# Edge weights of a tensor product kept as six blocks instead of four, and one VectorE product of 512 columns instead of two

## The chip, the cores and the metric

The kernel runs on one core of one Trainium2 chip. The metric is the device time of one execution in microseconds (us); lower is better. Several executions of the kernel before were timed, and one was recorded by the hardware profiler.

## The reference, cut to what matters

A graph of 6250 nodes and 100000 edges, sorted by destination, goes through four layers, each with a residual: a graph convolution with a mixture-of-experts feed-forward (64 experts, top 2), a SAGE layer (neighbour mean), a GCN layer, and a tensor product layer. All is float32. The change concerns the last layer and the weights of its edges:

```
h = silu(edge_scalars @ fc_w1 / sqrt(8)) * 1.679
w = h @ fc_w2 / sqrt(64)                      # 100000 x 256: blocks w_a, w_b, w_c, w_d of 64
xg0, xg1 = y0[edge_src], y1[edge_src]         # 64 and 64 x 3: one gathered row of 256
mid0 = w_a * xg0 * ea0
mid1 = w_b * sum_c(xg1[c] * ea1[c]) / sqrt(3)
mid2 = (w_c * xg0) * ea1                      # 64 x 3
mid3 = (w_d * ea0) * xg1                      # 64 x 3
agg  = segment_sum([mid0, mid1, mid2, mid3], edge_dst)   # 512 columns a node
```

## The kernel before, in words

The edges are cut into 832 windows of up to 128 edges (WINDOWS, 16 windows to a step, 52 steps), each window belonging to one tile of 125 nodes. Every layer first writes a table of 6250 rows of 256 values to HBM (`table_stage`) and then goes over the 832 windows.

`aggregate` (L628 on) does this for the first three layers. For each window GpSimd (POOL) gathers 128 rows of the table by an indirect DMA (L692), VectorE (DVE) makes the one-hot matrix of the destinations (`match`, L712), TensorE (PE) multiplies it with the gathered rows into a PSUM bank (L805), and DVE adds the bank to the node sums in SBUF (`add`, L724). The gathers run through a ring of 16 message buffers; `stage` (L705) hands POOL the indices of four windows at a time. Beside this, `aggregate` makes the edge weights of the *last* layer: in batches of 384 edges, SP loads the scalars and attributes (L865, L866), PE multiplies them (`first_product`, L781), ScalarE (ACT) applies silu (L824), PE multiplies by `fc2` (`second_product`, L788, three per batch, 256 columns each), ACT copies the result into `made`, half of it scaled by an edge attribute (`keep`, L833 and L834, 128 columns each), and SP stores `made` to `edge_rows` in HBM (L871), ROW = 260 values an edge. A batch goes with eight windows. The weights of `fc2` are loaded at the start of each `aggregate` by SP, block by block (L859), and scaled by DVE (L753, L754), for which PE waits before its first matmul. The third `aggregate` also stores its one-hot matrices to HBM (`kept_hots`, L876). The batches are spread over the three: 104 in the first, 104 in the second, the other 54 in the third.

`tensor_product_edges` (L1624 on) is the last pass over the windows. For each window:

- SP loads 128 rows of `edge_rows` into one of 6 weight buffers (L1665), and every fourth window four one-hot matrices (L1654). It waits until the product six windows back is done.
- POOL gathers 128 rows of `table3`, 256 values each, into one of 12 buffers (L1677), ahead of the others; every fourth window it waits until the products of the windows whose buffers it takes are done.
- ACT makes three scaled copies of the one-hot matrix (L1691).
- DVE forms the message of 512 columns in two products (`multiply`): L1727 makes the 2 blocks that take `xg0` (128 columns), L1729 the 6 blocks that take the three parts of `xg1` (384 columns).
- PE multiplies the message by the one-hot matrices in 8 passes (L1704, L1708), and DVE adds the bank of 512 columns to the sums (`add`, L1742).

The order on DVE is written out by `staggered`: the product of window w + 2, then the sum of window w. There are 3 message buffers and 8 banks. Sync is by semaphores set by hand; each engine runs its own list in order. Each window has the first edge that the tables give it; the last windows of the 832 have no edges left, and all of them read the same padding rows.

## Time and profile before

| | us |
|---|---|
| median of 3 runs (lowest, highest) | 6108.55 (6105.67, 6122.41) |
| the profiled execution, its own time | 6108.57 |
| its span, from the first instruction to the last | 6106.9 |
| PE, DVE, POOL, ACT busy in it | 5235.0, 3703.0, 3712.4, 1915.1 |

The stages, by the instructions of each in the trace: preparation to about 359 us, first `aggregate` to 1410, experts and batch norm to 2530, second table and `aggregate` to 3660, third to 4815, fourth table to 4932, `tensor_product_edges` from there to 6021, and the output stage to the end. The busy shares are averages over stages with different limits: what a stage is bound by is read from the windows of that stage, not from this table.

How a page is read: "busy" is the time in which an engine executes; "idle before" is the time just before an instruction in which its engine did nothing, and what ended it; "issue" means that nothing which the profile shows was waited for. PEclk is the granted TensorE clock as a share of 2.4 GHz. DMA share is the mean busy share of the 16 DMA engines; as packets of several queues can overlap, it can pass 1.00.

### The profile page before, as it was taken

The page shows a single profiled execution, that of the slowest core. Times are in us where ns is not written, and L with a number is a line of the kernel's source. Part 1 is how long each engine was busy: PE and PEld are TensorE (multiplying, and loading weights), DVE is VectorE, ACT ScalarE, POOL GpSimd, SP SyncE. Part 2 cuts the span into 40 slices and gives each one's busy share as a digit, 9 for nine tenths or more (in the row PEclk, how much of TensorE's full clock was granted, in tenths as well). Part 3 has the DMA queues.
Part 4 walks back from the last instruction along what each step waited for, and adds up shares of the span by engine and source line. Part 5 has one row for each costly group of instructions (what it writes and reads, how often), then busy time and mean ns, then how long its engine had stood idle before and what let it go on. Part 6 is the DMA issues. An engine that isn't in the chain of part 4 may idle for free. (4 is left out here: it accounts for less than half of the span.)

```text
span 6106.9 us, 94754 instructions
## 1 busy us (share of the span) xinstructions
PE 5235.0 (86%) x22327; PEld 3459.7 (57%) x22327; DVE 3703.0 (61%) x11360; ACT 1915.1 (31%) x5997; POOL 3712.4 (61%) x3961
## 2 busy tenths in 40 slices
PE   3589999996599995689999988899777689999998
PEld 2554444444388884444444445444333478888887
DVE  8746666666711112555555544555555579999997
ACT  0142222221022220422222214222000377777775
POOL 0147777771066661377777764777777557777771
PEclk9988888885799997788888877877776699999998
DMA  3145555554199993155555564666555468888884
GB/s 150 37 129 147 147 148 145 149 145 75 55 324 322 319 319 139 48 143 146 147 149 147 147 127 122 199 197 199 168 158 156 91 202 260 258 260 259 260 259 109
DMA packets 692159, 1062.44 MB, mean 174 GB/s; under 512 B 210437, under 2 KB 532051, under 8 KB 690970
## 3 DMA queue, kind: packets, MB, share of 16 engines
q0 software_dynamic: 180864, 480.03, 29.5%
q1 hardware_dynamic: 504383, 565.43, 28.9%
q10 hardware_dynamic: 6460, 12.03, 0.6%
q8 instruction: 151, 2.47, 0.2%
q14 instruction: 301, 2.47, 0.1%
HBM read 826.26 MB, written 236.47 MB: 174 GB/s over the span
## 5 line engine op out<-in xcount | busy, mean ns | idle before, releaser
L692 POOL DMA_INDIRECT agg_msg<-table,agg_idx x2496 | 2363.2, 947 | 842.5 <-issue 676.1
L805 PE MATMUL bank<-agg_msg,agg_hots 128*125 128x256 f32 (+1 forms) x4992 | 1910.9, 501 | 336.0 <-DMA agg_msg<-table,agg_idx 201.5
L805 PEld LDWEIGHTS bank<-agg_msg,agg_hots 128*125 128x125 f32 x4992 | 973.1, 228 | 1256.4 <-DVE agg_hots L712 669.3
L724 DVE TENSOR_TENSOR acc<-acc,bank 125x256 f32 x2496 | 1052.2, 422 | 1013.8 <-PE bank L805 971.3
L1677 POOL DMA_INDIRECT tp_src<-table,tp_idx x832 | 805.8, 968 | 300.2 <-issue 251.9
L1691 ACT ACTIVATE tp_hots<-tp_hot,tp_weight 128x125 f32<-128x125 f32 x2496 | 813.2, 390 | 281.2 <-PE bank L1708 238.5
L712 DVE TENSOR_SCALAR agg_hots<-iota_i,dst_w 128x126 f32<-128x126 f32 x2496 | 760.0, 305 | 0.0
L1708 PEld LDWEIGHTS bank<-tp_msg,tp_hots 128*125 128x125 f32 x4992 | 681.2, 189 | 47.1
L1708 PE MATMUL bank<-tp_msg,tp_hots 128*125 128x128 f32 x4992 | 685.8, 274 | 0.0
L833 ACT ACTIVATE agg_made<-bank,agg_made 128x128 f32<-128x128 f32 x786 | 288.6, 367 | 1255.6 <-PE bank L788 1253.3
L788 PE MATMUL bank<-agg_fc,agg_hid 64*128 64x256 f32 x1572 | 664.6, 509 | 0.0
L1742 DVE TENSOR_TENSOR acc<-acc,bank 125x512 f32 x832 | 594.0, 714 | 3.5 <-issue 1.6
L1704 PE MATMUL bank<-tp_msg,tp_hot 128*125 128x256 f32 x1664 | 559.8, 418 | 31.2 <-DVE tp_msg L1729 30.1
L1729 DVE TENSOR_TENSOR tp_msg<-tp_weight,tp_src 128x384 f32<-128x384 f32 x832 | 486.9, 585 | 0.0
L788 PEld LDWEIGHTS bank<-agg_fc,agg_hid 64*128 64x128 f32 x1572 | 278.4, 221 | 336.4 <-issue 336.4
L1511 DVE COPY ffn_res<-bank 128x256 f32<-128x256 f32 x162 | 68.8, 425 | 536.4 <-PE bank L1476 368.4
L723 DVE TENSOR_TENSOR deg_in<-deg_in,bank 125x1 f32 x832 | 130.7, 157 | 415.0 <-PE bank L805 387.2
L1428 POOL DMA_INDIRECT ffn_rows<-tokens,moe_token_of x162 | 157.7, 974 | 333.5 <-issue 333.5
L824 ACT ACTIVATE agg_hid<-bank 64x384 f32<-64x384 f32 x262 | 126.6, 483 | 724.9 <-PE bank L781 724.9
L1489 ACT ACTIVATE ffn_hid<-bank,ffn_b 128x128 f32<-128x128 f32 x648 | 184.6, 368 | 475.0 <-PE bank L1465 468.4
L1465 PE MATMUL bank<-ffn_cols,acc 128*128 128x128 f32 x2592 | 318.2, 277 | 3.0 <-DMA acc<-in_L_gnn_w_dram 2.2
L1704 PEld LDWEIGHTS bank<-tp_msg,tp_hot 128*125 128x125 f32 x1664 | 246.0, 187 | 124.1 <-issue 42.5
(285 smaller groups left out, 5407.5 us busy)
## 6 DMA issues: line engine op xcount, KB each, us to landing
tp_weight<-edge_rows SPq DMA_DIRECT2D x832, 130.0 KB
edge_rows<-agg_made SPq DMA_DIRECT2D x262, 390.0 KB, 3.5
acc<-in_L_w_laid_dram SPq DMA_DIRECT2D x162, 512.0 KB
acc<-in_L_gnn_w_dram SPq DMA_DIRECT2D x162, 512.0 KB
kept_hots<-agg_hots SPq DMA_DIRECT2D x208, 252.0 KB, 2.6
tp_hot<-kept_hots SPq DMA_DIRECT2D x208, 252.0 KB, 4.0
agg_msg<-table,agg_idx POOLq DMA_INDIRECT x2496, 2.9
table<-tab_out SPq DMA_DIRECT2D x40, 625.0 KB
```

Source lines behind the costliest of these rows:

```text
L692: pool.indirect_dma_start(out=msg[PER * g + r][:, 0:D], out_offset=None, in_=table[:, :], in_offset=bass.IndirectOffsetOnAxis(ap=idx[g][:, ...
L712: dve.tensor_scalar(hot[r % HOTS], net.iota_i[:, 0:HOT_W], net.dst_w[:, ds(WPI * i + r, 1)], None, ALU.is_equal).then_inc(s_hot, 1)
L724: dve.tensor_tensor(row, row, bank[0:P, 0:D], ALU.add).then_inc(s_add, 1)
L788: pe.matmul(wb[n % 2][:, 0:4 * MUL], hid[j % 2][:, c * Q:(c + 1) * Q], fc2[:, :, :].rearrange("p b n -> p (b n)"), start=True, stop=True). ...
L805: pe.matmul(net.bank[w % BANKS][0:P, 0:sums], hot[w % HOTS][:, 0:P], msg[w][:, :], start=True, stop=True).then_inc(s_sum, 1)
L1465: mm = pe.matmul(hidden[b % 2][:, j * Q:(j + 1) * Q], w1[b % R][:, c, j * Q:(j + 1) * Q], cols[b % 2][:, c, :], start=(c == 0), stop=(c == ...
L1677: pool.indirect_dma_start(out=src[w % R][:, :], out_offset=None, in_=table[:, :], in_offset=bass.IndirectOffsetOnAxis(ap=idx[w // WPI % 2] ...
L1691: ins = act.activation(hots[w % RM][:, c, :], hot[w // BLOCK % RB][:, w % BLOCK, 0:P], ACT.Copy, scale=weight[w % RW][:, 4 * MUL + 1 + c:4 ...
L1704: pe.matmul(out[:, 0:4, :], hot[w // BLOCK % RB][:, w % BLOCK, 0:P], m[:, 0:4, :], start=True, stop=False, skip_group_check=True)
L1708: mm = pe.matmul(out[:, 4 + c:8:3 - c, :], hots[w % RM][:, c, :], m[:, 4:6 + c:1 + c, :], start=False, stop=(c == 2), skip_group_check=True)
L1729: dve.tensor_tensor(quad, bc(wv[:, 2:4, :], 2, [Q, 2, 3, MUL]), bc(sv[:, 1:4, :], 1, [Q, 2, 3, MUL]), ALU.mult).then_inc(s_msg, 1)
L1742: dve.tensor_tensor(row, row, banks[w % len(banks)][0:P, :], ALU.add).then_inc(s_add, 1)
```

## The change

The weights of an edge are stored as six blocks of 64 instead of four, two of them twice (`fc2_of` = 0, 3, 3, 2, 1, 1), so ROW is 388 values instead of 260. With an access pattern that reads them as blocks 0, 1, 1, 2 and 3, 4, 4, 5, one product of 512 columns makes the whole message. In `aggregate`, `second_product` has 384 columns instead of 256, ACT's two copies 192 instead of 128, two more blocks of `fc2` are loaded, and the attributes stand behind the sixth block. In the first two `aggregate` the one-hot ring has 6 buffers instead of 8, each a tensor of its own, made 5 windows ahead instead of 6; in the third the ring of 16 lies in the unused half of the accumulator's tensor.

```
--- before.py
+++ after.py
@@ -54,7 +54,8 @@
...
 MUL = 64
-ROW = 4 * MUL + 4
+WIDE = 6
+ROW = WIDE * MUL + 4
 LN_EPS = 1e-5
...
@@ -635,13 +636,18 @@
...
     AHEAD = 12
-    HOTS, HOT_AHEAD = 8 if kept_hots is None else 16, 6
+    HOTS, HOT_AHEAD = (6, 5) if kept_hots is None else (16, 6)
     KEPT = HOTS // BLOCK
...
         msg = [ph.sb(f"msg{r}", [Q, sums]) for r in range(WPI)]
-        hots = [ph.sb(f"hots{r}", [Q, BLOCK, HOT_W]) for r in range(KEPT)]
-        hot = [hots[r // BLOCK][:, r % BLOCK, :] for r in range(HOTS)]
+        if kept_hots is None:
+            hot = [ph.sb(f"hot{r}", [Q, HOT_W])[:, :] for r in range(HOTS)]
+        else:
+            size = BLOCK * HOT_W
+            hots = [net.acc_full[:, T * D + r * size:T * D + (r + 1) * size].rearrange("p (b n) -> p b n", n=HOT_W)
+                    for r in range(KEPT)]
+            hot = [hots[r // BLOCK][:, r % BLOCK, :] for r in range(HOTS)]
         s_stored = [ph.sem(f"stored{r}") for r in range(KEPT)]
...
@@ -658,7 +664,7 @@
...
         first_batch, count = batches
-        fc1, fc2 = ph.sb("fc1", [8, MUL]), ph.sb("fc2", [MUL, 4, MUL])
+        fc1, fc2 = ph.sb("fc1", [8, MUL]), ph.sb("fc2", [MUL, WIDE, MUL])
         scal = [ph.sb(f"scal{b}", [8, BATCH * Q]) for b in (0, 1)]
...
@@ -666,7 +672,8 @@
...
         zb, wb = net.bank[BANKS + 1], net.bank[BANKS + 2:BANKS + 4]
-        fc2_of = (0, 2, 3, 1)
+        fc2_of = (0, 3, 3, 2, 1, 1)
+        FC_LOADS = 1 + len(fc2_of)

...
@@ -709,7 +716,7 @@
...
                         dve.wait_ge(s_stored[group % KEPT], 16 * (group // KEPT))
-                    dve.tensor_scalar(hot[r % HOTS], net.iota_i[:, 0:HOT_W], net.dst_w[:, ds(WPI * i + r, 1)], None,
+                    dve.tensor_scalar(hot[(WPI * i + r) % HOTS], net.iota_i[:, 0:HOT_W], net.dst_w[:, ds(WPI * i + r, 1)], None,
                                       ALU.is_equal).then_inc(s_hot, 1)
...
@@ -748,10 +755,11 @@
...
                 dve.sem_inc(s_add, BANKS)
-                dve.wait_ge(s_fc, 16 * 5)
-
-                dve.tensor_scalar(fc2[:, 0:3, :], fc2[:, 0:3, :], 1.679 * MUL ** -0.5, None, ALU.mult).then_inc(s_fcs, 1)
-                dve.tensor_scalar(fc2[:, 3, :], fc2[:, 3, :], 1.679 * MUL ** -0.5 * 3 ** -0.5, None, ALU.mult).then_inc(s_fcs, 1)
+                dve.wait_ge(s_fc, 16 * FC_LOADS)
+
+                dve.tensor_scalar(fc2[:, 0:4, :], fc2[:, 0:4, :], 1.679 * MUL ** -0.5, None, ALU.mult).then_inc(s_fcs, 1)
+                dve.tensor_scalar(fc2[:, 4:6, :], fc2[:, 4:6, :], 1.679 * MUL ** -0.5 * 3 ** -0.5, None,
+                                  ALU.mult).then_inc(s_fcs, 1)
                 if degrees:
...
@@ -785,10 +793,10 @@
...
                         pe.wait_ge(s_made, n - 1)
-                    pe.matmul(wb[n % 2][:, 0:4 * MUL], hid[j % 2][:, c * Q:(c + 1) * Q],
+                    pe.matmul(wb[n % 2][:, 0:WIDE * MUL], hid[j % 2][:, c * Q:(c + 1) * Q],
                               fc2[:, :, :].rearrange("p b n -> p (b n)"), start=True, stop=True).then_inc(s_w, 1)

-                pe.wait_ge(s_fc, 16 * 5)
+                pe.wait_ge(s_fc, 16 * FC_LOADS)
                 pe.wait_ge(s_fcs, 2)
...
@@ -802,7 +810,7 @@
...
                         pe.wait_ge(s_msg[w], 16 * i + 16)
-                        pe.matmul(net.bank[w % BANKS][0:P, 0:sums], hot[w % HOTS][:, 0:P], msg[w][:, :],
+                        pe.matmul(net.bank[w % BANKS][0:P, 0:sums], hot[(WPI * i + w) % HOTS][:, 0:P], msg[w][:, :],
                                   start=True, stop=True).then_inc(s_sum, 1)
...
@@ -826,12 +834,13 @@
...
                     n = BATCH * j + c
-                    to, of = (m.rearrange("p (k h n) -> p k h n", k=2, h=2)
-                              for m in (made[j % 2][:, c, 0:4 * MUL], wb[n % 2][:, 0:4 * MUL]))
+                    half = WIDE // 2 * MUL
+                    to, of = made[j % 2][:, c, :], wb[n % 2]
                     act.wait_ge(s_w, n + 1)
                     act.wait_ge(s_in[j % 2], 32 * (j // 2) + 32)
-                    act.activation(to[:, :, 0, :], of[:, :, 0, :], ACT.Copy, scale=made[j % 2][:, c, 4 * MUL:4 * MUL + 1])
-                    act.activation(to[:, :, 1, :], of[:, :, 1, :], ACT.Copy).then_inc(s_made, 1)
+                    act.activation(to[:, 0:half], of[:, 0:half], ACT.Copy,
+                                   scale=made[j % 2][:, c, WIDE * MUL:WIDE * MUL + 1])
+                    act.activation(to[:, half:2 * half], of[:, half:2 * half], ACT.Copy).then_inc(s_made, 1)

...
@@ -863,7 +872,7 @@
...
                     sp.dma_start(scal[j % 2][:, :], net.scal_t[:, rows_of(j)]).then_inc(s_in[j % 2], 16)
-                    sp.dma_start(made[j % 2][:, :, 4 * MUL:ROW],
+                    sp.dma_start(made[j % 2][:, :, WIDE * MUL:ROW],
                                  net.attr[rows_of(j), :].rearrange("(c p) k -> p c k", p=Q)).then_inc(s_in[j % 2], 16)
...
@@ -1689,7 +1698,7 @@
...
                         ins = act.activation(hots[w % RM][:, c, :], hot[w // BLOCK % RB][:, w % BLOCK, 0:P], ACT.Copy,
-                                             scale=weight[w % RW][:, 4 * MUL + 1 + c:4 * MUL + 2 + c])
+                                             scale=weight[w % RW][:, WIDE * MUL + 1 + c:WIDE * MUL + 2 + c])
                     ins.then_inc(s_hots, 1)
...
@@ -1721,13 +1730,11 @@
...
                         dve.wait_ge(s_sum, w - RM + 1)
-                    m = msg[w % RM][:, :, :]
-                    wv = weight[w % RW][:, 0:4 * MUL].rearrange("p (b n) -> p b n", n=MUL)
-                    sv = src[w % R][:, :].rearrange("p (b n) -> p b n", n=MUL)
-                    dve.tensor_tensor(m[:, 0:8:4, :], wv[:, 0:2, :], sv[:, 0:1, :].broadcast_to([Q, 2, MUL]), ALU.mult)
-                    quad = m.rearrange("p (g k) n -> p g k n", g=2)[:, :, 1:4, :]
-                    dve.tensor_tensor(quad, bc(wv[:, 2:4, :], 2, [Q, 2, 3, MUL]),
-                                      bc(sv[:, 1:4, :], 1, [Q, 2, 3, MUL]), ALU.mult).then_inc(s_msg, 1)
+                    row = weight[w % RW][:, :]
+                    overlapping = bass.AP(row.tensor, row.offset, [list(row.ap[0]), [3 * MUL, 2], [MUL, 2], [MUL, 2], [1, MUL]])
+                    sv = src[w % R][:, :].rearrange("p (h k n) -> p h k n", h=2, k=2)
+                    dve.tensor_tensor(msg[w % RM][:, :, :].rearrange("p (g h k) n -> p g h k n", g=2, h=2), overlapping,
+                                      bc(sv, 1, [Q, 2, 2, 2, MUL]), ALU.mult).then_inc(s_msg, 1)

```

## Rows read from the trace of the kernel before

**Rows 1.** Stretches: each engine's busy us and instructions, granted clock, DMA share, GB/s.
```profile
core 0: us, PE busy (x) PEld busy (x) DVE busy (x) ACT busy (x) POOL busy (x), PEclk, DMA share, GB/s
370.00:1340.00 970.00, 918.10 (x2595) 470.79 (x2594) 597.85 (x2494) 218.74 (x722) 730.63 (x772) 0.82 0.54 147
...
4300.00:4770.00 470.00, 351.31 (x756) 165.80 (x756) 252.12 (x871) 0.53 (x2) 355.47 (x377) 0.68 0.52 158
4938.00:4944.00 6.00, 5.97 (x32) 5.31 (x31) 3.85 (x10) 4.41 (x15) 4.60 (x5) 0.75 0.97 317
5000.00:5900.00 900.00, 897.51 (x5644) 779.71 (x5643) 898.77 (x2161) 689.49 (x2116) 684.79 (x707) 1.00 0.87 260
...
5965.00:6010.00 45.00, 30.77 (x151) 26.24 (x151) 25.67 (x60) 18.23 (x57) 20.48 (x22) 0.73 0.93 147
```

**Rows 2.** Timeline of DVE in the last pass: start us, us, instruction.
```profile
5499.44 0.71 DVE L1742 TENSOR_TENSOR acc<-acc,bank 125x512 f32 x1
5500.03 0.31 DVE L1727 TENSOR_TENSOR tp_msg<-tp_weight,tp_src 128x128 f32<-128x128 f32 x1
5500.23 0.58 DVE L1729 TENSOR_TENSOR tp_msg<-tp_weight,tp_src 128x384 f32<-128x384 f32 x1
5500.70 0.71 DVE L1742 TENSOR_TENSOR acc<-acc,bank 125x512 f32 x1
```

**Rows 3.** Timeline of POOL in the third aggregate.
```profile
4499.66 0.94 POOL L692 DMA_INDIRECT agg_msg<-table,agg_idx  x1 [0.30 <-issue]
4500.91 0.95 POOL L692 DMA_INDIRECT agg_msg<-table,agg_idx  x1 [0.30 <-issue]
```

**Rows 4.** Timeline of POOL in the last pass, near its start and in its middle.
```profile
4955.36 0.94 POOL L1677 DMA_INDIRECT tp_src<-table,tp_idx  x1 [0.30 <-issue]
4956.61 0.94 POOL L1677 DMA_INDIRECT tp_src<-table,tp_idx  x1 [0.30 <-issue]
...
5499.40 0.96 POOL L1677 DMA_INDIRECT tp_src<-table,tp_idx  x1 [0.30 <-issue]
5500.67 0.97 POOL L1677 DMA_INDIRECT tp_src<-table,tp_idx  x1 [0.30 <-issue]
```

**Rows 5.** All gathers of the last pass: duration ns min/median/max, first and last start; landing.
```profile
L1677 POOL DMA_INDIRECT tp_src<-table,tp_idx x832: 940/964/1200, 4932.8 to 6005.7; - x167
...
DMA to landing us min/median/max: 3.2/4.0/16.0
```

**Rows 6.** Waits between 5000 and 5900 us: us in total, times, longest.
```profile
POOL tp_src L1677 <- issue: 215.2, 706, 0.3
ACT tp_hots L1691 <- PE bank L1708: 206.0, 694, 0.9
...
PE bank L1704 <- DVE tp_msg L1729: 1.5, 5, 0.6
...
DVE tp_msg L1727 <- DMA tp_src<-table,tp_idx: 0.3, 1, 0.3
```

**Rows 7.** Timeline of PE's weight loads in the last pass.
```profile
5501.25 0.84 PEld L1708 LDWEIGHTS bank<-tp_msg,tp_hots 128*125 128x125 f32 x6
5502.20 0.29 PEld L1704 LDWEIGHTS bank<-tp_msg,tp_hot 128*125 128x125 f32 x2
```

**Rows 8.** DMA between 5000 and 5900 us.
```profile
DMA packets 161021, 233.57 MB, mean 260 GB/s; under 512 B 25416, under 2 KB 138277, under 8 KB 160887
...
q1 hardware_dynamic: 126968, 139.43, 51.4%
q0 software_dynamic: 33919, 92.66, 34.9%
```

**Rows 9.** A stretch of the experts stage (columns as in Rows 1).
```profile
1662.00:1682.00 20.00, 17.08 (x105) 15.08 (x106) 2.87 (x8) 5.74 (x17) 7.49 (x10) 0.86 1.03 411
```

**Rows 10.** Costliest groups that the edge weights take in the three aggregates.
```profile
L833 ACT ACTIVATE agg_made<-bank,agg_made 128x128 f32<-128x128 f32 x786 | 288.6, 367 | 1255.6 <-PE bank L788 1253.3
L788 PE MATMUL bank<-agg_fc,agg_hid 64*128 64x256 f32 x1572 | 664.6, 509 | 0.0
```

**Rows 11.** The first aggregate's start: SP's loads of fc2, then DVE's first sum.
```profile
358.74 2.43 SPq L859 DMA_DIRECT2D agg_fc<-in_L_gnn_fc_w_dram  x4
...
365.20 0.42 DVE L724 TENSOR_TENSOR acc<-acc,bank 125x256 f32 x1
```

## The prediction

> **What bounds the kernel now.** I read the busy shares of stretches first [rows 1]. Between 5000 and 5900 us, inside the last pass, DVE is busy 898.77 of 900 us and PE 897.51, while 707 windows pass: 900 / 707 = 1.273 us a window. Both look full, so the next view is the timeline of DVE [rows 2]: from the start of one sum (L1742) to the first product 0.59 us, from that to the second product 0.20, from that to the next sum 0.47; together 1.26 to 1.27, and no gap. A DVE instruction of 512 columns holds the next one back 0.59 to 0.60, one of 128 columns 0.20, one of 384 columns 0.47. That is 64 + columns, divided by 0.96 a ns: 0.600, 0.200, 0.467, sum 1.267. Nobody delays DVE: in those 900 us it waited 0.3 us for a gather, and PE waited for it [rows 6]. PE has a little room: its weight loads of one window end at 5502.09 and the next begin at 5502.20, 0.11 us later, which leaves PE about 1.27 - 0.11 = 1.16 us of its own a window [rows 7]. So DVE sets the pace, PE comes with 1.16.
>
> Two resources stand just below that pace. The first is **POOL**. In the third aggregate a gather takes 0.94 to 0.95 us, then POOL is idle 0.30 waiting for nothing that the profile shows, and the next begins 1.25 us after the last [rows 3]. That holds where DVE, PE and the DMA engines all have room: DVE busy 252 of 470 us, DMA share 0.52, and POOL still does 377 gathers in 470 us, 1.247 us each [rows 1]. So 1.25 us is POOL's own cost of a gather, and all three aggregates are bound by it. In the last pass POOL begins with the same 1.25 and then goes 1.27 [rows 4]; it looks idle 0.30 before each of the 706 gathers, but those are the same 0.30 [rows 6]. POOL is nearly full too, and has 0.023 us to give. The second is the **DMA engines**: share 0.87 at 260 GB/s [rows 1].
>
> **The change, part by part.** The sum is made against the profiled execution's own 6108.57 us (span 6106.9 and 1.7 around it); the median is 6108.55, the same.
>
> 1. *One product instead of two.* By the rule read above, two instructions hold DVE 0.200 + 0.467 = 0.667 us, one of 512 columns 0.600. DVE's own window falls from 1.267 to 1.200, 0.067 less. The pattern has five dimensions and overlaps, which no row shows; the bounds are that it runs at the rate of the others (0.600) or gives everything back (0.667). I take 0.600, since both products of today already read with repeats and keep that rate.
> 2. *What is late next.* POOL, at 1.25. DVE overtakes it: today's lead of some windows is used up at 0.05 us a window, and from then on DVE waits for the gather. The steady part loses 1.273 - 1.250 = 0.023 us a window and not 0.067. It has the windows from 4937 to 5965 us, 1028 / 1.273 = 808: **-18.6 us**. PE's 1.16 lies below 1.25, and ACT's three copies are busy 689.49 / 707 = 0.98 us a window [rows 1]; both stay covered.
> 3. *Bytes of the last pass.* Today 233.57 MB / 707 = 330 kB a window [rows 8]. A row grows by 128 values, so a window by 128 x 512 B = 65.5 kB, to 396 kB. At 1.25 us that is 317 GB/s. What can the engines do? The lower bound is today's share taken as full use: 260 / 0.87 = 299 GB/s, which gives 1.32 us a window. The upper is the experts stage, 411 GB/s in packets of another size, 0.96 us [rows 9]. Nearest is the start of this very pass, where the queues were full of the same kinds of packets: 317 GB/s at a share of 0.97, so 327, or 1.21 us [rows 1]. I take this one: DMA stays just below POOL, at zero cost. The number of instructions on SP is the same.
> 4. *The padding windows.* From 5965 to 6010 us the DMA share is 0.93 at only 147 GB/s, and the engines wait for data [rows 1]. The other 24 windows fall mostly here, with 24 x 65.5 kB = 1.57 MB more. At 147 GB/s that is 10.7 us; at 317 GB/s 5.0; if the slow part is only the gathers of one repeated row, near 0. I take **+5**, ends 0 and +11.
> 5. *The aggregates, DMA.* Stores grow from 390 to 582 kB a batch; at a share of 0.54 [rows 1] that is hidden, except at the end of the first two, whose last windows gather a repeated row as well. Ends 0 and +7 each; I take 2 each, **+4**.
> 6. *The aggregates, PE and ACT.* L788 goes from 256 to 384 columns. Half of 509 ns [rows 10] for six passes a batch is 1.5 us in the 10 us that eight windows take. PE is idle only 970 - 918 = 52 of 970 us, 0.5 in 10, but that is at a granted clock of 0.82; the same work at 1.00 would leave 18% more, 1.8 us. Without the weights (4300 to 4770) PE is busy 351 of 470 us at 0.68, and POOL goes at the same pace [rows 1], so slack on PE does not speed the pass. The ring of 16 messages takes up the stretches at the low clock. I take 0; if that cover fails, 1.0 us a batch of 262 is open, +260 at the very worst. ACT's copies get 64 columns more, on an engine busy 219 of 970 us: 0.
> 7. *The aggregates' start.* Two more loads of fc2 at 2.43 / 4 = 0.6 us each on SP [rows 11] delay PE's first matmul by 1.2 us, three times; the loads of scalars and attributes queue behind them. POOL has 12 gathers to do before it needs the first sum, 12 x 1.25 = 15 us from about 359, and the first sum is at 365.2 [rows 11]: hidden, 8 us to spare; without it, 3.6 us in all.
> 8. *The one-hot rings.* Six buffers, made five windows ahead: PE can be at most four banks ahead of DVE's sums, so it asks for nothing that isn't made. The wait on the stored groups in the third stays as it was. 0.
>
> Sum: 6108.6 - 18.6 + 5 + 4 = **6099 us**. With every small cost at zero 6090; with them at their ends (-18.6 + 11 + 14) 6115.
>
> **The rivals.** About 0.3%, 18 us, is what a measurement of this kernel can tell from no change.
>
> *A. As above, POOL takes over.* 6090 to 6115. For it: the even 1.25 in 2496 gathers of the aggregates. Chance 0.57; in a fifth of it the costs come out at zero and the time falls just under 6090.
>
> *B. The gathers are held back by the longer product.* POOL starts at 1.25 in this pass and then falls into step with DVE: at 5500.67 a gather begins just where the second product gives DVE free (5500.23 + 0.47 = 5500.70), and its duration has gone from 0.94 to 0.97 [rows 2, 4]. No aggregate shows that, where DVE has no instruction with two inputs in SBUF. So something in a gather waits for the products. Today the two leave a seam between them; one of 0.600 us has none. While DVE is the slower one this is harmless, since POOL just follows. Once DVE waits for the gathers, a product stands where its data landed, 4.0 us after the issue in the median today [rows 5], more under the heavier load. The fourth gather after it begins at 4 x 1.25 = 5.0 us. If landing takes over 4.4, the product (0.6) is still running then, and the gather waits: the window becomes (landing + 0.6) / 4, 1.275 at 4.5 us, 1.35 at 4.8. It decides from 4.4 us on; at 1.31 it costs 808 x 0.037 = +30, and with the small costs 6148. Against it: at 4.0 it is free. Chance 0.19, a third of it inside 0.3%.
> The Trainium skill speaks against the change here: "SBUF — State Buffer", section "SBUF: two separate sides", has VectorE with two SBUF inputs and GpSimd exclude each other from a shared port pair for a whole instruction. By that rule a gather may stand up to one product, 0.6 us; the trace agrees that there is a coupling, with 0.02 us a gather today.
>
> *C. DMA becomes the bound.* If a share of 0.87 is nearly all that random rows allow, the window is 1.32 us: 808 x 0.05 = +40, and with the small costs 6155; at 1.29, 6130. For it: 0.87 is high, and gathers landed within 4.0 us against a best of 3.2. Against it: 317 GB/s at the start of the pass. It decides where the window passes 1.273, below 311 GB/s. Chance 0.14, a fourth of it inside 0.3%.
>
> *D. PE becomes the bound of the aggregates.* A tenth of the open 260 us is +26: 6125. Chance 0.04.
>
> *E. The gather's 1.25 is not a floor*, and DVE's 0.067 comes in full: 808 x -0.067 = -54, 6064 with the small costs. Against it: 706 gathers with no more than 0.3 us before each. Chance 0.03. That the product gains nothing (0.667) leaves 6108.6 + 9 = 6118: chance 0.03, inside 0.3%.
>
> **How the numbers follow.** The point is A's, 6099. Faster by over 0.3%: E and a fifth of A, 0.03 + 0.11, rounded up to 0.15. Slower: two thirds of B, three fourths of C and D, 0.13 + 0.10 + 0.04, and A's upper end with two of these together, 0.30. The rest, 0.55, within 0.3%. The range of 8 in 10 leaves E out and the upper halves of B and C: 6087 to 6150. A's own range is 6090 to 6115.
>
> **What would show it.** If A holds, the last pass's steady part has 720 windows in 900 us, POOL's gathers begin 1.25 apart with 0.94 to 0.95 each, DVE's timeline shows the sum and one product of 0.60 each and then some 0.05 us of waiting for the gather, and the DMA share is 0.95 or more at about 317 GB/s. B would show gathers of over 1.0 us, or gaps on POOL over 0.30, with DVE waiting for gathers. C would show DVE and ACT waiting for the weights' loads, a share of 1.0, and POOL waiting for products. D would show fewer than 80 gathers in 100 us in the first two aggregates. E would show gathers less than 1.24 apart. The forecast is wrong if the steady window is outside 1.24 to 1.27.

## The result and the profile after

The changed kernel took 6194.35 us (median of 4 runs, 6157.36 to 6214.83) against 6111.86 for the kernel before, measured beside it (6105.67 to 6122.41): a ratio of 1.0126, 95% interval 1.0076 to 1.0177. By that ratio it is slower by 77 us (the medians lie 82 apart), and its runs differ among themselves by 57 us where those of the kernel before differ by 17. Measured again beside other runs it gave 1.0108 (1.009 to 1.0126). Its profiled execution took 6196.68 us (span 6195.1, 88.2 longer than before's). Runs classed as slow are left out of the ratios here and below: one each of the kernels of numbers 8 (6271.81 us) and 13 (6277.91), and two of the kernel before (7943 and 23924).

First the same stretches as in [rows 1], of the changed kernel: the busy time of each engine with its count, then the granted clock, the DMA share and GB/s.

```profile
370.00:1340.00 970.00, 937.47 (x2482) 449.51 (x2481) 572.01 (x2386) 238.45 (x690) 695.53 (x736) 0.83 0.54 158
2620.00:3640.00 1020.00, 964.89 (x2663) 471.01 (x2662) 510.92 (x1779) 247.20 (x717) 721.11 (x762) 0.84 0.55 159
4300.00:4770.00 470.00, 365.39 (x824) 170.75 (x823) 251.69 (x868) 22.28 (x65) 352.89 (x373) 0.72 0.55 169
5100.00:6000.00 900.00, 897.88 (x5761) 795.61 (x5760) 897.82 (x1486) 701.43 (x2161) 680.70 (x721) 1.00 0.97 317
```

The last line is the part that the change is about: 721 gathers in 900 us, 1.248 us a window where it was 1.273, at the 317 GB/s and the share of 0.97 that step 3 had worked out. The first line is the loss. In the same 970 us of the first aggregate POOL makes 736 gathers and made 772 before [rows 1]; 970 / 736 is 1.318 us each, no longer 1.25. The second aggregate shows the same, 762 gathers where the kernel before had 815:

```profile
2620.00:3640.00 1020.00, 949.11 (x2716) 481.56 (x2716) 542.14 (x1867) 210.29 (x707) 770.01 (x815) 0.84 0.55 146
```

(this line alone is of the kernel before). One more way to see it is to take each pass from its first gather to its last, the last two times of these lines. Of the changed kernel:

```profile
L699 POOL DMA_INDIRECT agg_msg<-table,agg_idx x832: 940/946/1017, 359.1 to 1454.0; - x167
L699 POOL DMA_INDIRECT agg_msg<-table,agg_idx x832: 940/946/1008, 2651.3 to 3727.2; - x167
L699 POOL DMA_INDIRECT agg_msg<-table,agg_idx x832: 941/946/1004, 3844.2 to 4889.2; - x167
L1686 POOL DMA_INDIRECT tp_src<-table,tp_idx x832: 941/946/1352, 5025.8 to 6079.2; - x167
```

Of the kernel before, for the first three (the fourth is in [rows 5]):

```profile
L692 POOL DMA_INDIRECT agg_msg<-table,agg_idx x832: 940/946/1010, 358.8 to 1403.0; - x167
L692 POOL DMA_INDIRECT agg_msg<-table,agg_idx x832: 940/946/1004, 2598.9 to 3641.1; - x167
L692 POOL DMA_INDIRECT agg_msg<-table,agg_idx x832: 940/946/1006, 3755.2 to 4796.2; - x167
```

| first to last gather, us | 1st aggregate | 2nd | 3rd | last pass |
|---|---|---|---|---|
| before | 1044.2 | 1042.2 | 1041.0 | 1072.9 |
| changed | 1094.9 | 1075.9 | 1045.0 | 1053.4 |
| difference | +50.7 | +33.7 | +4.0 | -19.5 |

The gathers of the aggregates themselves are no longer (median 946 ns in both). The passes add up to +68.9. Another 14.7 us come after the last gather. That part took between 98 and 125 us in the profiled executions of all kernels here, 101 in the kernel before and 125 in the one that differs from it in the rings alone, so these 14.7 can't be told from its scatter. Between the passes there are 4.3 us and at the start 0.4.

**Where POOL stands in the aggregates.** The waits between 400 and 1400 us, of the changed kernel:

```profile
POOL agg_msg L699 <- issue: 203.6, 661, 1.1
POOL agg_msg L699 <- DVE agg_idx L712: 80.7, 95, 5.6
```

and of the kernel before:

```profile
POOL agg_msg L692 <- issue: 217.0, 706, 1.9
POOL agg_msg L692 <- DVE agg_idx L705: 30.0, 90, 1.3
```

POOL waits for DVE's `stage` as often as before, but for up to 5.6 us and 51 us more in all. `stage` isn't slow: DVE makes it in its turn between the sums, and the sums wait for PE. Such a wait in the timeline of POOL (start, duration, and in brackets the idle time before), then a sum of DVE that PE holds back and the `stage` (L712) that comes two sums later and releases POOL:

```profile
684.87 0.95 POOL L699 DMA_INDIRECT agg_msg<-table,agg_idx  x1 [0.30 <-issue]
689.41 0.94 POOL L699 DMA_INDIRECT agg_msg<-table,agg_idx  x1 [3.60 <-DVE agg_idx L712]
```

```profile
685.16 0.16 DVE L730 TENSOR_TENSOR deg_in<-deg_in,bank 125x1 f32 x1 [1.79 <-PE bank L813]
688.46 0.16 DVE L712 COPY agg_idx<-src_w 128x4 f32<-128x4 f32 x1
```

What PE does around it, in short stretches of the changed kernel (columns as above):

```profile
675.00:680.00 5.00, 5.00 (x10) 2.41 (x9) 2.55 (x11) 0.64 (x2) 3.78 (x4) 0.50 0.37 107
680.00:685.00 5.00, 5.00 (x9) 2.01 (x8) 1.46 (x6) 1.28 (x4) 2.96 (x4) 0.50 0.27 79
685.00:690.00 5.00, 5.00 (x11) 2.59 (x10) 2.82 (x13) 0.48 (x1) 1.41 (x2) 0.50 0.60 175
690.00:695.00 5.00, 5.00 (x13) 2.00 (x11) 2.96 (x14) 1.28 (x4) 3.31 (x5) 0.77 0.32 89
695.00:702.00 7.00, 7.00 (x26) 3.82 (x24) 4.67 (x20) 1.72 (x5) 5.00 (x6) 1.00 0.59 176
```

PE is full, 5.00 of 5.00, at a granted clock of 0.50, which is 1.2 GHz, and POOL makes 2 gathers in a stretch where it could make 4. With the clock back at 1.00 (2.4 GHz) POOL is on its pace again. The kernel before has such stretches too, but gets through them, for example here:

```profile
420.00:425.00 5.00, 5.00 (x10) 2.77 (x10) 2.39 (x10) 0.81 (x3) 3.78 (x4) 0.50 0.38 105
425.00:430.00 5.00, 5.00 (x10) 2.30 (x10) 1.57 (x7) 1.27 (x6) 3.81 (x4) 0.50 0.36 105
430.00:435.00 5.00, 5.00 (x16) 2.68 (x15) 3.37 (x15) 0.48 (x1) 3.42 (x4) 0.80 0.67 187
```

The ring of 16 messages nearly lasts until the clock comes back: of the gathers from 405 to 440 us one, at 434.42, is late, by 0.6 us. The matmuls of the weights at the low clock, before (415 to 430 us) and changed (668 to 690 us), in that order; the last two numbers are busy us and mean ns:

```profile
L788 PE MATMUL bank<-agg_fc,agg_hid 64*128 64x256 f32 x6 | 3.7, 710 | 0.0
```

```profile
L796 PE MATMUL bank<-agg_fc,agg_hid 64*128 64x384 f32 x6 | 4.9, 926 | 0.0
```

A batch's six passes hold PE for 4.9 us where it was 3.7, in a stretch where it has nothing to spare. Gathers that began more than 1.4 us after the one before, counted in POOL's timeline and called late from here on: before 6, 2 and 1 in the three aggregates, worth 7 us beyond 1.25 each; changed 32, 20 and 4, worth 95. They go with the low clock: of the changed kernel's 56 late gathers 33 have a granted clock of 0.50 in the 5 us before them, and 55 have at most 0.74 over the 20 us before them; the nine of the kernel before have 0.54 to 0.63 there. The third aggregate, which has half as many batches and no root products on PE, is spared.

That is rival D, which had a chance of 0.04 and a price of 26 us. No run holds the clock fixed, so that the low clock is what turns the additional columns into late gathers is read from these rows and not tested by itself. Four parts of the change lie in the aggregates, though: 384 columns on PE, 192 instead of 128 in ACT's copies, rows of 388 to store, and the rings. The experiments take them apart.

### The profile page after: what moved, and what is told of

Same layout as the page of the kernel before. It is cut to its first block and busy times, and to the rows that moved or that the text cites. A ratio compares the mean times of both kernels' runs of the same rounds, so it can differ in the third digit from the quotient of the medians.

```text
span 6195.1 us, 93928 instructions
## 1 busy us (share of the span) xinstructions
PE 5364.8 (87%) x22327; PEld 3460.6 (56%) x22327; DVE 3679.0 (59%) x10528; ACT 1995.6 (32%) x5997; POOL 3694.4 (60%) x3961
## 5 line engine op out<-in xcount | busy, mean ns | idle before, releaser
L731 DVE TENSOR_TENSOR acc<-acc,bank 125x256 f32 x2496 | 1052.0, 421 | 1050.8 <-PE bank L813 1003.6
L813 PE MATMUL bank<-agg_msg,agg_hot 128*125 128x257 f32 (+1 forms) x3328 | 1161.6, 469 | 112.7 <-DMA agg_msg<-table,agg_idx 53.5
L813 PEld LDWEIGHTS bank<-agg_msg,agg_hot 128*125 128x125 f32 x3328 | 626.8, 215 | 809.6 <-DVE agg_hot L719 393.9
L1686 POOL DMA_INDIRECT tp_src<-table,tp_idx x832 | 787.4, 946 | 299.1 <-issue 248.9
L796 PE MATMUL bank<-agg_fc,agg_hid 64*128 64x384 f32 x1572 | 861.4, 634 | 0.0
L813 PE MATMUL bank<-agg_msg,acc 128*125 128x256 f32 x1664 | 677.0, 528 | 170.4 <-DMA agg_msg<-table,agg_idx 112.6
L841 ACT ACTIVATE agg_made<-bank,agg_made 128x192 f32<-128x192 f32 x786 | 330.4, 420 | 1348.0 <-PE bank L796 1344.5
L813 PEld LDWEIGHTS bank<-agg_msg,acc 128*125 128x125 f32 x1664 | 340.0, 241 | 552.9 <-DVE acc L719 352.0
L1736 DVE TENSOR_TENSOR tp_msg<-tp_weight,tp_src 128x512 f32<-128x512 f32 x832 | 596.3, 717 | 32.9 <-issue 17.7
L1749 DVE TENSOR_TENSOR acc<-acc,bank 125x512 f32 x832 | 561.9, 675 | 3.5 <-PE bank L1717 1.8
L719 DVE TENSOR_SCALAR agg_hot<-iota_i,dst_w 128x126 f32<-128x126 f32 x1664 | 516.2, 311 | 0.0
```

The costliest lines, as they stand in the source:

```text
L719: dve.tensor_scalar(hot[(WPI * i + r) % HOTS], net.iota_i[:, 0:HOT_W], net.dst_w[:, ds(WPI * i + r, 1)], None, ALU.is_equal).then_inc(s_ho ...
L731: dve.tensor_tensor(row, row, bank[0:P, 0:D], ALU.add).then_inc(s_add, 1)
L796: pe.matmul(wb[n % 2][:, 0:WIDE * MUL], hid[j % 2][:, c * Q:(c + 1) * Q], fc2[:, :, :].rearrange("p b n -> p (b n)"), start=True, stop=Tru ...
L813: pe.matmul(net.bank[w % BANKS][0:P, 0:sums], hot[(WPI * i + w) % HOTS][:, 0:P], msg[w][:, :], start=True, stop=True).then_inc(s_sum, 1)
L841: act.activation(to[:, 0:half], of[:, 0:half], ACT.Copy, scale=made[j % 2][:, c, WIDE * MUL:WIDE * MUL + 1])
L1686: pool.indirect_dma_start(out=src[w % R][:, :], out_offset=None, in_=table[:, :], in_offset=bass.IndirectOffsetOnAxis(ap=idx[w // WPI % 2] ...
```

## The experiments

Ratios are to the kernel before, measured beside each (medians 6112 to 6121 us); "single" is one profiled execution without an interval. Every pass length is from the first gather to the last, in one profiled execution of each kernel, and for the kernel before it is the table's unless another is named. Of each edit only the lines that carry it are shown, and "..." stands for what is left out within a line.

**1. The rings alone.** Kernel before with the changed one-hot rings.

```
-    HOTS, HOT_AHEAD = 8 if kept_hots is None else 16, 6
+    HOTS, HOT_AHEAD = (6, 5) if kept_hots is None else (16, 6)
```

> The kernel before with the changed one-hot rings alone (6 buffers, 5 windows ahead in the first two aggregates; the third's ring in the accumulator's tensor). If TensorE's additional columns made the aggregates longer, this one is the kernel before: gathers of the first aggregate over 1044 us, of the second over 1042, the whole within 0.3% of 6112. If the shorter ring did it, the first aggregate takes about 1095 and the second 1076, and the whole about 6190.

1.0003 (0.9991 to 1.0014), passes of 1044.4, 1045.8, 1042.4 and 1067.2 us. Step 8 holds. The rings are in most of the kernels below.

**2. The rings and 384 columns.** `fc2` gets two more blocks, PE multiplies by all six, ACT and the rows stay as before.

```
-                    pe.matmul(wb[n % 2][:, 0:4 * MUL], hid[j % 2][:, c * Q:(c + 1) * Q],
+                    pe.matmul(wb[n % 2][:, 0:6 * MUL], hid[j % 2][:, c * Q:(c + 1) * Q],
```

> The last one with 384 columns in the second product of the edge weights instead of 256; ScalarE still copies 256 of them, edge rows stay 260 values, the last pass stays as before. If TensorE's columns are the cause, the first two aggregates take about 1095 and 1076 us and the whole about 6190 to 6200; POOL's long gaps (over 1.4 us) number some 20 to 25 in each, waiting for indices that DVE hands out after TensorE's sums. If the longer copies on ScalarE or the larger stores are the cause, this stays at 6112.

1.0077 (1.006 to 1.0095): the columns alone cost some 45 us, (1.0077 - 1.0003) x 6115. The passes are 1051.1, 1071.9, 1043.8 and 1069.6, with 8 and 21 late gathers in the first two. That is about half of what was expected of the columns: the second aggregate is nearly as long as in the changed kernel, the first is not, so the columns alone are not the whole loss.

**3. PE as before, ACT doubles the blocks.** Changed kernel, but PE multiplies 256 columns and ACT makes four copies (128, 64, 128, 64 columns) instead of two. The last pass is the changed one.

```
+                    act.activation(to[:, 0:2 * MUL], of[:, 0:2 * MUL], ACT.Copy, scale=scale)
+                    act.activation(to[:, 2 * MUL:half], of[:, MUL:2 * MUL], ACT.Copy, scale=scale)
+                    act.activation(to[:, half:half + 2 * MUL], of[:, 2 * MUL:4 * MUL], ACT.Copy)
+                    act.activation(to[:, half + 2 * MUL:2 * half], of[:, 3 * MUL:4 * MUL], ACT.Copy).then_inc(s_made, 1)
```

> The changed kernel with 256 columns on TensorE again; ScalarE writes the two doubled blocks by two more copies (four per 128 edges instead of two). If TensorE's columns are the cause, the aggregates return to about 1044 and 1042 us (stores as large as in the changed kernel, ScalarE busier than in it) and the whole comes to about 6112 - 16 = 6096, faster than both. If stores or ScalarE are the cause, it stays at 6190 or gets worse.

1.0009 (0.9998 to 1.002), passes 1052.9, 1059.3, 1040.0, 1058.4. Without the wide product most of the loss is gone. The aggregates did not come back to 1044 and 1042, as was expected: they still take 25 us longer than before, which eats the last pass's 14.5. The larger rows (number 5) and the additional copies (number 6) stand in this kernel too.

**4. The changed kernel with the two products of before in the last pass** (read as blocks 0, 3 and 1, 4 of the wide rows).

```
-                    dve.tensor_tensor(msg[w % RM][:, :, :].rearrange(...), overlapping, bc(sv, 1, [Q, 2, 2, 2, MUL]), ALU.mult)
+                    dve.tensor_tensor(m[:, 0:8:4, :], wv[:, :, 0, :], sv[:, 0:1, :].broadcast_to([Q, 2, MUL]), ALU.mult)
+                    dve.tensor_tensor(quad, bc(wv[:, :, 1, :], 2, [Q, 2, 3, MUL]), bc(sv[:, 1:4, :], 1, ...), ALU.mult)
```

> The changed kernel with the two products of 128 and 384 columns in the last pass, reading the six stored blocks. The aggregates are as in the changed kernel. In the last pass DVE sets the pace again: 1.273 us a window, 707 in 900 us, DMA share about 0.95 at 311 GB/s, POOL in step at 1.27; the padding windows as long as in the changed kernel. If the DMA engines rather than POOL's gathers set the changed kernel's 1.25, this shows no more waits for loads either, since it asks for less.

Single: 6201.23 us. The last pass is back at 1073.6, while the aggregates keep their loss (1086.1, 1068.5). So the one product is what shortens the last pass, by 20 us, and it has no part in the loss.

**5. The larger rows.** Kernel before with the rings and rows of 388 values, of which two blocks are zero; 256 columns, two products.

```
-ROW = 4 * MUL + 4
+ROW = 6 * MUL + 4
```

> The kernel before with the changed rings and rows of 388 values in the buffers, the stores and the last pass's loads; the two additional blocks are zero, TensorE has 256 columns and ScalarE its two copies of 128, the last pass its two products. If stores cost the aggregates their time, these take some 8 and 17 us longer and the whole is about 6140. If the copies on ScalarE did, the aggregates take 1044 and 1042, and the whole is about 6115 to 6120 (some us from the padding windows).

1.0027 (1.0018 to 1.0036), 15 us over the rings alone: passes 1052.0, 1049.1, 1040.9 and 1073.9. Against the kernel before, the bytes cost 8 and 7 us in the first two aggregates (8 and 3 against number 1) and 1 in the last pass, whose first 790 windows take 1006.0 us, as before.

**6. Four copies on ACT**, two of them into a place that nobody reads, rows of 260.

```
+                    act.activation(made[j % 2][:, c, ROW:ROW + MUL], of[:, 1, 0, :], ACT.Copy, scale=...)
+                    act.activation(made[j % 2][:, c, ROW + MUL:ROW + 2 * MUL], of[:, 1, 1, :], ACT.Copy)
```

> The kernel before with the changed rings and four copies on ScalarE per 128 edges instead of two; the two additional ones go to places that are not stored, and everything else is as before. If ScalarE's copies hold TensorE back (it waits for the bank of the product before the last), the first two aggregates take some 8 and 17 us longer, the whole about 6140. If not, 1044 and 1042 and 6115.

1.0009 (1.0 to 1.0017), up to 4 us over the rings.

**7. The doubling by the stores.** Aggregates of before, four stores a batch write the blocks to their places in rows of 388; changed last pass.

```
+                    for at, of, size in ((0, 0, 2 * MUL), (2 * MUL, MUL, MUL), (3 * MUL, 2 * MUL, 2 * MUL), (5 * MUL, 3 * MUL, MUL + 4)):
+                        sp.dma_start(to[:, :, at:at + size], made[j % 2][:, :, of:of + size])...
```

> The kernel before in the aggregates (256 columns on TensorE, two copies of 128 on ScalarE, one-hot ring of 8), but each batch is stored by four DMAs that write two of the four blocks twice into rows of 388; the last pass is the changed kernel's. If TensorE's columns and ScalarE's copies made the aggregates longer, they return to 1044, 1042 and 1041 us, and the last pass keeps its 1053: the whole about 6112 - 16 = 6096, ratio 0.997. If the larger stores made part of it, the first two stay 8 to 17 us longer, as with the blocks doubled by ScalarE, and the whole is about 6120.

1.0022 (1.001 to 1.0034): 1049.8, 1054.5, 1042.0, then 1060.2. Also without a single column more on PE or ACT the aggregates' passes lose 19 us in all (expected were none, or 8 and 17 in the first two if the larger stores cost something), and the last pass gives back 13. Another 12 us lie between the passes, behind the first two aggregates.

**8. Both extras of the aggregates, without the new last pass.** Rings, rows of 388 and 384 columns; copies of 128; two products.

> The kernel before with the rings, rows of 388 numbers (two blocks zero) and products of 384 columns in the aggregates, copies of 128 numbers, and the two products of before in the last pass: both extras of the aggregates at once. If the parts only add, +45 us for the columns and +15 us for the rows give a ratio of about 1.010 (6175 us). If they add up to more together, it is 1.013 or more (6195 us), since the last pass brings nothing back here and the changed kernel with its 18 us back stands at 1.011.

1.0165 (1.0127 to 1.0203), about 100 us; the medians, 6207.24 and 6120.37, lie 87 apart. Columns and rows together cost more than their single prices, 45 + 15. Less the last pass's 20 this gives 67 to 80 for the changed kernel, which showed 66 to 77. These 87 to 100 belong to the time; its one profiled execution was its shortest run (6172.83) and shows 15, 32, 9 and 1 us on the four passes.

**9. Still more columns.** Kernel before with the rings and 512 columns in `second_product`, rows of 260.

```
+                    pe.matmul(wb[n % 2][:, 0:8 * MUL], hid[j % 2][:, c * Q:(c + 1) * Q],
```

> The kernel before with the changed rings and 512 columns in the second product (256 of them used); the dose beside 384. In proportion to the columns it would cost twice the 45 us, 6205. If the ring of 16 messages first takes up the lag and then no longer, it is clearly over twice: with 34 us stretches at a granted clock of 0.5 in which POOL waits more than half of the time, 6230 to 6290.

1.0075 (1.005 to 1.0101), far below what was expected (6205 at least): no more than with 384 columns. Its four runs lie between 6125 and 6175, and the profiled one is the shortest (6125.15), with 1047.1 and 1040.1 us in the first two aggregates. The first aggregate of this kernel, and then of number 2:

```profile
370.00:1340.00 970.00, 947.24 (x2611) 430.57 (x2611) 599.13 (x2513) 219.96 (x726) 728.29 (x771) 0.93 0.53 146
```

```profile
370.00:1340.00 970.00, 928.98 (x2582) 445.70 (x2581) 594.14 (x2485) 218.01 (x717) 730.58 (x770) 0.87 0.53 146
```

The granted clock is 0.93, 0.87, and 0.82 before [rows 1]; in the second aggregate it is 0.94, 0.84 and 0.84. Over whole executions, in every run of each, it is 0.881 to 0.893 with 512 columns, 0.860 to 0.865 with 384, and 0.847 to 0.857 with 256 (number 1), so in this series PE spends less time at 1.2 GHz the more columns it has. The changed kernel does not follow: it has 384 columns and the larger rows, and 0.83 in its first aggregate. That the price does not grow with the columns because stretches at the low clock become fewer is the reading that fits these numbers; no run tests it.

**10. Is POOL the bound of the new last pass, or are it the bytes?** Two changed kernels that compute something else. One loads one-hot matrices for the first 16 windows alone and reuses them; the other gathers for every second window alone and uses each gather twice.

```
-                        sp.wait_ge(s_sum, BLOCK * (g - RB + 1))
+                        return
```

> The changed kernel with only the first 16 windows' one-hot matrices loaded in the last pass and used again for all, so the sums of later windows are not those of the reference. 64.5 kB of 396 kB a window are not moved. If POOL's 1.25 us a gather sets the last pass, the window stays 1.25 us (720 in 900 us) while the DMA share falls from 0.97 to about 0.80 at 265 GB/s. If the DMA engines set it, the window falls towards VectorE's 1.20, 750 in 900 us.

```
+                    if w % 2:
+                        continue
```

> The changed kernel with a gather for every second window only in the last pass; the window between takes the same 128 rows, so its sums are not those of the reference. It takes half of POOL's work and 65 kB of 396 kB a window away. If POOL's gather is the floor of the last pass, the window falls from 1.25 us to VectorE's two instructions of 512 columns, 1.20 to 1.21 us (664 windows in 800 us), or to TensorE if that needs more. If it stays at 1.25, TensorE or the DMA engines are the floor.

Singles, 6180.56 and 6102.16 us. The stretch from 5100 to 5900 us of the first and of the second:

```profile
5100.00:5900.00 800.00, 799.18 (x5110) 705.71 (x5110) 799.38 (x1318) 624.96 (x1917) 605.20 (x640) 1.00 0.89 265
```

```profile
5100.00:5900.00 800.00, 799.42 (x5304) 732.28 (x5303) 799.32 (x1369) 647.06 (x1989) 365.05 (x332) 1.00 0.90 274
```

With 52 GB/s less (a share of 0.89, where 0.80 was expected) the window is still 800 / 640 = 1.25. With half the gathers it is 1.21 (5304 / 8 = 663 windows). POOL's gathers are the bound, not the DMA engines, and the next one is DVE, at just the 1.20 of step 1, as the second kernel's timeline of DVE shows:

```profile
5499.17 0.68 DVE L1739 TENSOR_TENSOR tp_msg<-tp_weight,tp_src 128x512 f32<-128x512 f32 x1
5499.77 0.67 DVE L1752 TENSOR_TENSOR acc<-acc,bank 125x512 f32 x1
5500.37 0.68 DVE L1739 TENSOR_TENSOR tp_msg<-tp_weight,tp_src 128x512 f32<-128x512 f32 x1
```

**11. The changed kernel once more**, to have its variation beside the runs above.

> The changed kernel once more, beside the others of this call, so that its distance has the same base as theirs. So far the parts by themselves gave, against the kernel before: rings 0, TensorE's 384 columns +45, four copies instead of two +4 (an upper bound for the two longer ones), rows of 388 with their padding windows +15, the last pass's window of 1.25 about -18. Added up: +46, 6160, ratio 1.0075. If the parts add more than that together (TensorE, held up at its low clock, is also the one that the other parts delay), it is 6180 to 6200, ratio 1.010 to 1.014.

1.0108 (1.009 to 1.0126), runs of 6161 to 6191 us, passes of 1077.9, 1060.8, 1045.8 and 1054.4.

**12. Batches moved off the root products.** 80, 78 and 104 batches over the aggregates instead of 104, 104 and 54, in three kernels: the one of number 3, the kernel before, the changed kernel.

```
-        aggregate(net, "agg0", table0, degrees=True, batches=(0, 2 * STEPS),
+        aggregate(net, "agg0", table0, degrees=True, batches=(0, 80),
```

> The kernel with 256 columns and four copies, the batches of edge weights now spread 80, 78 and 104 over the three aggregates instead of 104, 104 and 54. The third has no root products on TensorE and took 1040 us with its 54 batches. If the root products are what fills TensorE up, the first two come to about 1046 us each and the third stays at 1042, the last pass at 1056: the whole about 6100, ratio 0.998. If the low-clock stretches cost as much in the third, nothing is gained: 6123.

> The kernel before with nothing changed but the batches: 80, 78 and 104 over the three aggregates. If what a batch costs beside the root products is only the gaps of the kernel before (4.3 us in 89 batches, 2.0 in 87), moving brings under 3 us, and the ratio is 0.9995 to 1.000; the 0.997 of moved_batches is then the last pass's 18 us. If moving alone does it, it is 0.997.

> The changed kernel (384 columns, rows of 388) with the batches 80, 78 and 104. If its cost lies in the batches beside root products alone, a tenth of it goes: 1.010 to 1.011. If the third aggregate has idle TensorE time for all and low clock comes only of a high load, up to half of it goes: about 1.005.

0.997 (0.9959 to 0.9981), 0.9976 (0.9963 to 0.9989) and 1.0042 (1.0023 to 1.0062). The changed kernel gets back more than half of its loss, from 66 or 77 us to 26. Some 15 of that are not the columns', though, since the surprise is the kernel before: 15 us faster, though its four passes are as long as ever (1044.5, 1041.2, 1040.3, 1072.3). The gain lies **behind** the gathers of an aggregate. Kernel before, end of the first one, in stretches and in the waits between 1409 and 1424 us:

```profile
1403.00:1410.00 7.00, 5.96 (x11) 2.48 (x10) 2.53 (x11) 1.07 (x4) 0.93 (x1) 0.50 0.98 73
1410.00:1420.00 10.00, 0.00 (x0) 0.00 (x0) 0.46 (x2) 0.00 (x0) 0.00 (x0) 0.50 0.97 108
1420.00:1430.00 10.00, 8.82 (x22) 4.45 (x22) 3.76 (x15) 2.08 (x7) 0.00 (x0) 0.74 0.04 12
```

```profile
PE bank L781 <- DMA agg_made<-attr: 10.9, 1, 10.9
```

PE does nothing for 10 us: its list has a batch's first product next, and the load for it stands behind the gathers of the padding windows, with the DMA share at 0.97 and only 108 GB/s. The load was issued at 1403.8, when the store of rows issued at 1390.7, whose buffer it takes, had landed after 12.7 us; the product began at 1420.5, 16.7 us later. The next store, issued at 1406.3, took 15.2 us to land. Once batches are left for the last steps of the third aggregate alone, the wait is only there: 11.82 us before one sum, where the first two have none over 1.5.

**13. No batches in the last four steps of any aggregate**: 96, 96 and 70, in the kernel before and in that of number 3.

> The kernel before with the batches 96, 96 and 70, so that none falls into the last four steps of any aggregate. In the kernel before PE stood 11 us at the end of the first aggregate and 12 us at the end of the second, for the load of a batch's scalars behind the gathers of the padding windows; before_moved took both away but set one of 12 us at the end of the third. If that stall is what the moving brought, here all are gone: about 24 us, ratio 0.996 (6096 us), better than before_moved. If it was the moving away from the root products that helped, only a tenth or less of the batches moves here, and the ratio is 0.999 to 1.000.

> The one product of 512 columns with ACT doubling the blocks (256 columns on PE), and the batches 96, 96 and 70. If the end stalls are the whole gain of moved_batches, the ratio is act_twice's 1.0009 less 24 us: 0.997. If the last pass's 14 to 18 us come through on top of before_early, it is 0.993 to 0.994. Low-clock gaps of the first two aggregates (20 us more than before in act_twice) decide which.

0.9958 (0.9944 to 0.9971) and 0.9967 (0.9955 to 0.9979). The kernel before with this one edit takes 6090.67 us; 25 us are gone, as expected, one wait of 12 or so in each of the first two aggregates. At the same place it now shows

```profile
1410.00:1420.00 10.00, 7.20 (x13) 2.96 (x12) 3.50 (x13) 0.00 (x0) 0.00 (x0) 0.50 0.65 60
```

so relief of the root products has little to do with it, as only 16 batches move. It beats both kernels and is at least as good as the one with the single product: that has 1058.9 instead of 1073.1 us in the last pass, but 1059.0 and 1058.5 instead of 1045.6 and 1044.6 in the first two aggregates.

## Why the prediction was wrong

By the prediction's steps:

- **Steps 1 and 2 (the product, POOL late next): right in size and in the bound.** 1.248 us a window against the 1.250 forecast, and the first 790 windows took 987.9 us where they took 1006.1: -18.2, forecast -18.6. Number 10 shows the gathers as the bound and DVE's own 1.20. How DVE is held to POOL's pace is not as forecast. It doesn't wait for the gather's data: from 5100 to 6000 us such waits add up to 1.5 us, and a product begins 6.25 us or more after its gather was issued, which landed after 4.8 us in the median. From the start of a product to the next sum it takes 0.65 instead of 0.60 us, and so it does where a gather begins at the same moment, as beside most of the products; where the gather begins 0.1 us or more earlier it takes 0.60, and its record is 0.68 instead of 0.73. So the 0.05 lie inside the product and come with the two beginning together. Without them DVE would gain 0.05 us a window and use up those 1.4 us in some 30 windows, so the pace would be POOL's all the same:

```profile
5498.62 0.73 DVE L1736 TENSOR_TENSOR tp_msg<-tp_weight,tp_src 128x512 f32<-128x512 f32 x1
5499.27 0.67 DVE L1749 TENSOR_TENSOR acc<-acc,bank 125x512 f32 x1
5499.87 0.73 DVE L1736 TENSOR_TENSOR tp_msg<-tp_weight,tp_src 128x512 f32<-128x512 f32 x1
```

- **Step 3 (bytes): right.** 317 GB/s at a share of 0.97. ACT waited for weights 61 times from 5100 to 6000 us, 35.1 us in all and no more than 1.9 in one, and DVE not at all. Rival C is out.
- **Step 4 (padding windows, +5): its lower end.** Whole pass -19.5, first 790 windows -18.2; number 5's wider rows lengthened the pass by 1 us. It is about 0.
- **Step 5 (the aggregates' transfers, +4): wrong in where it looked.** It let the rows cost something at the end of an aggregate alone. They cost 15 us by themselves (number 5), seen along the passes. At the ends little was added, 1.3 and 2.9 us between the passes of the changed kernel: the wait for the attributes' load, 12.83 us in DVE's timeline of the first before, is 9.93 in the changed kernel. That this wait was there at all was overlooked.
- **Step 6 (the aggregates' TensorE and ScalarE at 0): the step that failed.** It said "The ring of 16 messages takes up the stretches at the low clock". It does so for 256 columns and a row of 260 but for 7 us in all. With 384 columns it doesn't: +45 us alone, +87 to 100 with the larger rows. That the ring was near its end could be read from the trace of before: nine gathers were late there, all behind a stretch at the low clock. Two figures in the step misled. That the same work at 1.00 would leave 18% more is a mean over 970 us, and a mean over two levels says nothing of the stretch at the lower one, where PE is 5.00 of 5.00 busy. And that POOL keeps its pace without the weights says nothing of what happens with more of them: "slack on PE does not speed the pass" is true, but the lack of it slows the pass. The open term was put at +260 at the very worst, which held; a tenth of it at a chance of 0.04 was far too little.
- **Step 7 (loads of fc2) and step 8 (rings): right**, 0 each: the first gather starts at 359.1 and the pass after the rings' change is as long as before.

Of the rivals, **D** came true. Its sign, "fewer than 80 gathers in 100 us", was badly chosen: the first two aggregates have 75.9 and 74.7 now, but had 79.6 and 79.9 before, which is under 80 as well. It is the loss of 4 to 5 in 100 that shows it. **B** did not: from 5100 to 6000 us the median gather is no longer (946 ns, one of 721 over 1.0 us), and POOL is idle for no more than 0.30 before any. Its mechanism is real nevertheless. In the kernel of number 10 that gathers for every second window, a gather that falls beside a product, 0.26 us after its start, takes 0.30 longer, and so it goes in every second one of them:

```profile
5500.63 1.24 POOL L1688 DMA_INDIRECT tp_src<-table,tp_idx  x1 [2.31 <-DVE tp_msg L1739]
5502.17 0.95 POOL L1688 DMA_INDIRECT tp_src<-table,tp_idx  x1 [0.30 <-issue]
```

In the changed kernel most gathers start together with a product (5498.62 in both timelines) and have 0.95, and it is the product that is 0.05 longer, as told under step 2. This fits the rule of the Trainium skill, "SBUF — State Buffer", section "SBUF: two separate sides", that such a VectorE instruction and GpSimd exclude each other; but its price depends on how the two fall together, and in this kernel they fall so that it is nothing on the gather. The same section of the Trainium skill lets whichever starts first keep the ports for its whole instruction; a gather of 0.95 us that starts with a product lengthens it by 0.05 here, not by its whole length, and the measurement decides. That the shift is due to this rule was not tested by itself.

**Left open:** why the columns and the rows together cost some 27 to 40 us more than one by one. Both delay the return of a message buffer, and a wait longer than the ring is worth costs in full what a shorter one costs not at all; that is an argument, not a measurement. It is also open what sets the moments at which the clock is lowered, and with it the spread of 57 us among the runs.

## What to carry to other kernels

Work that is put beside a gather-bound pass is free only as long as the fullest engine gets through its worst stretch, so before costing more columns at zero read the stretches at the low clock, not the mean: the busy share there, and whether a gather is late behind them already. Try extras together, too: here two that cost 45 and 15 us cost 87 to 100 together. A saving in one pass that is paid for in the passes that prepare its data (here 19.5 us against 88 in the profiled execution) should be costed there first. And look behind the last gather of every pass: a load that an engine's list has next can stand behind a burst of slow transfers, and starting its work a few steps earlier gave 25 us, more than the change itself could have brought.

## What the runs showed of the hardware that was not expected

- With more columns on PE the granted TensorE clock was higher: over whole executions 0.847 to 0.857, 0.860 to 0.865 and 0.881 to 0.893 with 256, 384 and 512 columns (numbers 1, 2 and 9), and 512 columns cost no more than 384 (1.0075 and 1.0077). With the larger rows beside 384 columns it was 0.850 to 0.862 (the changed kernel). And a granted clock of 0.50 can stand while PE is busy without a gap: 5.00 us of every 5 from 410 to 430 us in the kernel before, and from 660 to 690 in the changed one.
- An indirect gather of 128 rows takes POOL 1.25 us wherever nothing holds it back, at DMA shares from 0.52 to 0.97, in all aggregates and the new last pass. A VectorE product with two inputs in SBUF that began 0.26 us before a gather made it 0.30 us longer; a gather that began together with a product made the product 0.05 longer.
- Gathers of one repeated row fill the DMA engines, a share of 0.97 at 108 GB/s. A store of rows issued among them took 15.2 us to land, where such stores have a median of 3.3, and the product that needed a load of 6 kB, issued 2.5 us before that store, began 16.7 us after the load's issue.
